# Gated cross-attention with experts: x and the experts' rows turned by VectorE out of 32-column quarters instead of by TensorE

## The chip, the core and the metric

The kernel runs on 1 core of one Trainium2 chip. A time is the device time of one execution in microseconds (us); the median of 3 runs is compared. One more execution is profiled, and all durations below come from it. TensorE (PE) multiplies, VectorE (DVE) and ScalarE (ACT) work on tiles in SBUF and PSUM, GpSimd (POOL) computes a little and issues the indexed transfers, and SyncE (SP) issues all other transfers, in the order in which its program names them.

## The reference, cut to what matters

```
x: (32, 128, 256)   ctx: (32, 128, 192)   16 heads of 64   8 experts, hidden 1024, capacity 1024
x = x + tanh(g_xattn) * attention(layernorm(x), ctx)          # Wq, Wk, Wv, Wo, bo
xf = layernorm(x) as (4096, 256)
each row goes to its two best experts' lists (first choices first, at most 1024 rows an expert)
h  = relu(rows @ fc1.T + b1);  eo = h @ fc2 + b2              # for each expert
x  = x + tanh(g_ffn) * sum over its two experts of gate * eo
```

All in float32. The kernel splits each float32 operand of a product into a high part (float32r) and the rest and adds three products.

## The kernel before, in words

**Attention.** The 32 batches are worked on in 8 groups `g` of 4 batches (`GB`), 512 tokens (`TOK`). A group has 8 steps `j`, one for each pair of heads; step `u = 8 g + j`. In step `u` TensorE turns the probabilities of step `u - 2`, makes the queries, the next keys and values, the scores of step `u`, and weighs values for step `u - 2`. VectorE takes maxima of the scores, copies turned probabilities out of PSUM, and scales probabilities (`scale_probs`, in two halves `hh`); ScalarE takes exponentials, which need the maxima. Single steps carry more (`misc_of`, line 77): `O0`, `O1` (output projection of the group before, step 2), `XA`, `XB`, `LT`, `LX`, `PR` (routing of the group before, steps 3 to 6), and in step 7 `FA` and `FB`: 4 transposes each, which turn the next group's normalised x, `xn`, into a PSUM bank (`front`, line 578). ScalarE then copies the bank to `xT_h`, VectorE subtracts to `xT_l` (line 1136), and the next query waits for both (`s_f_split`, line 523). `xn` itself is normalised by VectorE in place in step 5 (groups 0 and 1) or 4 (line 956). VectorE's order in step 7 is: maxima of the step before, `probs_out`, `scale_probs` half 0, `attention_low`, `route_slots` (from group 1 on), `scale_probs` half 1, the two subtractions for `xT_l`.

SP's order in the attention is a list by hand: `iteration(g, nxt, has_prev)` (line 282) loads x of group g + 1, the context of group g + 2, the x rows for the residual (into `rows[:, 1]`), and stores the finished x. After `iteration(0)` SP issues one transfer of 8256 KB that fills `disp`, the experts' lists in DRAM, with blanks (line 305); it waits for nothing but a memset.

**Experts.** 8 experts, each in two halves of 512 rows: groups `n = 0 .. 15`. A group has an up part (8 tiles `m` of 6 products of 512 columns), then 8 transposes that turn the rows of group n + 1 from `rows[half]` into the PSUM banks `rT` (`transpose_rows`, line 1353, called at line 1400), then a down part (96 products of 256 columns). ScalarE applies the Relu of each up tile, copies `rT` to `rT_h` (`high_rows`) and, once for each expert, copies the next expert's weights (`split_high`). VectorE splits `hid`, subtracts for `rT_l` (`low_rows`), subtracts for the weights (`split_low`), and writes the scaled result `eo`. GpSimd adds `eo` into the output by index. SP's `step(e, nxt, par)` (line 1285) loads the weights of expert `nxt` (`load_expert`), its biases, and then the rows of both halves, each of which waits until VectorE has read the tags of group n (`s_meta`), so the rows of group n + 2 are asked for at the start of group n.

## Time and profile before

| | us |
|---|---|
| median of 3 runs (lowest, highest) | 948.61 (948.35, 949.02) |
| the profiled execution | 951.25 |
| its span | 949.5 |
| PE busy | 930.2, 98% of the span |
| DVE, ACT, POOL busy | 651.6, 515.6, 276.7 |
| granted TensorE clock, mean | 0.997 of full |

The profiled execution took 951.25 us, 1.75 us more than the span from its first to its last instruction, and 2.64 us more than the median. Busy time of PE is modelled for pipelined products, so the step from one PE instruction's start to the next is what a product costs, and not its listed length.

### The profile page before, as it was taken

How to read it: one execution, taken by the hardware profiler on the slowest of the kernel's cores; microseconds unless marked ns; L12 is line 12 of the kernel's file. 1: busy time of each engine (PE TensorE's matmuls, PEld its weight loads, DVE VectorE, ACT ScalarE, POOL GpSimd, SP SyncE). 2: the span in 40 equal slices, each digit the busy share in tenths (PEclk: the TensorE clock that was granted, in tenths of full speed). 3: DMA queues.
4: the chain of work that ended last, by engine and by line, in shares of the span. 5: the costliest groups of instructions: out<-in, count | busy, mean ns of one | idle time of the engine just before them, and what ended most of it. 6: DMA issues, size and time to landing. Idle time of an engine off the chain costs nothing.

```text
span 949.5 us, 19031 instructions
## 1 busy us (share of the span) xinstructions
PE 930.2 (98%) x7224; PEld 813.0 (86%) x7224; DVE 651.6 (69%) x1536; ACT 515.6 (54%) x1608; POOL 276.7 (29%) x300
## 2 busy tenths in 40 slices
PE   8999999999999999999999999999999999999996
PEld 6788889889889888888898877999999999999995
DVE  4884895895885886867847747665757575757552
ACT  5774684784783774755847624343434343535331
POOL 4911133133133233243022250223232323232222
PEclk9999999999999999999999999999999999999998
DMA  9196320120021021012011015525252626252222
GB/s 250 36 295 141 111 68 29 40 73 34 30 79 57 1 79 58 14 58 65 13 35 46 33 70 169 139 45 139 46 142 42 148 43 148 45 146 48 29 23 23
DMA packets 61019, 73.36 MB, mean 77 GB/s; under 512 B 5870, under 2 KB 53781, under 8 KB 60928
## 3 DMA queue, kind: packets, MB, share of 16 engines
q1 hardware_dynamic: 48640, 55.89, 19.7%
q0 software_dynamic: 12288, 16.25, 9.5%
q8 instruction: 58, 0.95, 0.4%
q14 instruction: 33, 0.27, 0.1%
HBM read 43.23 MB, written 29.49 MB: 77 GB/s over the span
## 4 chain that ended last, share of the span: by engine, by line
PE 92%; DVE 2%; ACT 1%; issue 1%; DMA 1%; POOL 1%; another core or an unknown queue 0%; POOLq 0%; DVEq 0%; SPq 0%
PE out_bank L603 6%; PE probT L590 6%; PE down L1411 6%; PE down L1413 6%; PE down L1412 6%; PE score L615 6%; PE up L1395 6%; PE up L1394 6%; PE up L1396 6%; PE query_bank L531 3%; PE query_bank L533 3%; PE query_bank L532 3%; PE key_bank L557 3%; PE rT L1358 1%; PE key_bank L549 1%; PE key_bank L551 1%
## 5 line engine op out<-in xcount | busy, mean ns | idle before, releaser
L1447 ACT ACTIVATE hid<-up,b 128x512 f32<-128x512 f32 x124 | 85.4, 690 | 199.1 <-PE up L1396 126.1
L1330 POOL DMA_INDIRECT out_dram<-eo,index x64 | 99.7, 1559 | 274.9 <-DVE eo L1517 246.2
L1067 DVE TENSOR_REDUCE negmax<-score 128x4 f32<-128x512 f32 x128 | 82.3, 685 | 41.1 <-PE score L615 41.0
L430 POOL DMA_INDIRECT disp<-packed,slots x56 | 58.3, 1041 | 159.8 <-DMA disp<-packed,slots 105.7
L805 ACT ACTIVATE k_sb<-key_bank 128x512 f32<-128x512 f32 x64 | 38.7, 605 | 118.1 <-PE key_bank L557 116.9
L853 ACT ACTIVATE probs_odd<-score,negmax 128x128 f32<-128x128 f32 x256 | 91.3, 383 | 20.8 <-DVE negmax L1067 20.8
L853 ACT ACTIVATE work<-score,negmax 128x128 f32<-128x128 f32 x256 | 91.5, 385 | 16.7 <-DVE negmax L1067 16.1
L1508 DVE TENSOR_TENSOR hid_l<-hid,hid_h 128x512 fp32r<-128x512 f32 x128 | 88.7, 693 | 4.4
L1075 DVE COPY pT<-probT 128x512 f32<-128x512 f32 x128 | 82.3, 685 | 13.7 <-PE probT L590 13.5
L1517 DVE SCALAR_TENSOR_TENSOR eo<-down,gate,shares_b 128x256 f32<-128x256 f32 x64 | 29.6, 481 | 85.5 <-PE down L1413 85.5
L1506 DVE CAST hid_h<-hid 128x512 fp32r<-128x512 f32 x128 | 54.8, 428 | 37.6 <-ACT hid L1447 36.7
L615 PEld LDWEIGHTS score<-k_sb,q_sb 64*128 64x128 f32 x1024 | 66.7, 187 | 5.6 <-ACT q_sb L805 3.1
L1411 PE MATMUL down<-w_split,hid_h 128*128 128x256 f32 x256 | 71.3, 279 | 0.0
L1411 PE MATMUL down<-w_h,hid_h 128*128 128x256 f32 x256 | 71.3, 279 | 0.0
L1413 PE MATMUL down<-w_split,hid_l 128*128 128x256 f32 x256 | 70.7, 276 | 0.0
L1413 PE MATMUL down<-w_h,hid_l 128*128 128x256 f32 x256 | 70.7, 276 | 0.0
L1412 PE MATMUL down<-w_l,hid_h 128*128 128x256 f32 x256 | 70.7, 276 | 0.0
L1412 PE MATMUL down<-w_split,hid_h 128*128 128x256 f32 x256 | 70.7, 276 | 0.0
L603 PE MATMUL out_bank<-pT,v_sb 128*64 128x128 f32 x1008 | 68.9, 279 | 0.7 <-DVE aT_l L937 0.5
L615 PE MATMUL score<-k_sb,q_sb 64*128 64x128 f32 x1024 | 68.5, 273 | 1.0 <-ACT q_sb L805 0.9
L603 PEld LDWEIGHTS out_bank<-pT,v_sb 128*64 128x64 f32 x1008 | 53.7, 136 | 8.4 <-DVE aT_l L937 0.7
L853 ACT ACTIVATION_READ_ACCUMULATOR work<-score,negmax 128x1 f32 x256 | 57.3, 224 | 0.0
(314 smaller groups left out, 2753.6 us busy)
## 6 DMA issues: line engine op xcount, KB each, us to landing
disp<-fixed SPq DMA_DIRECT2D x1, 8256.0 KB, 34.2
rows<-disp SPq DMA_DIRECT2D x16, 516.0 KB, 5.0
rows<-x_dram SPq DMA_DIRECT2D x16, 512.0 KB, 5.2
w_raw<-fc1T_dram SPq DMA_DIRECT2D x8, 1024.0 KB, 8.0
w_raw<-fc_dram SPq DMA_DIRECT2D x8, 1024.0 KB, 10.7
out_dram<-rows SPq DMA_DIRECT2D x8, 512.0 KB
c_raw<-ctxT_dram SPq DMA_DIRECT2D x8, 256.0 KB, 4.4
c_raw<-ctxT_dram SPq DMA_DIRECT2D x16, 128.0 KB, 4.9
```

The source lines that it names most:

```text
L430: pool.indirect_dma_start(out=disp[:, :], out_offset=bass.IndirectOffsetOnAxis(ap=slots[:, j, b:b + 1], axis=0), in_=rows_[:, b, :], in_of ...
L603: last = mm(bank[hh * DH:(hh + 1) * DH, b * P:(b + 1) * P], v_sb[:, j // 4, b, cols], pT[:, hh, b * P:(b + 1) * P], start=True, stop=True)
L615: last = mm(score[hh][:, t], q_sb[r, t], k_sb[u % 2][r, t], start=True, stop=True)
L853: last = nc.scalar.activation(probs[w % 2][:, c, :], score[hh][:, b * P:(b + 1) * P], ACT.Exp, bias=negmax[:, w % 2, c:c + 1], accum_out=s ...
L1067: V.tensor_reduce(negmax[:, w % 2, hh * GB:(hh + 1) * GB], score[hh][:, :].rearrange("p (i k) -> p i k", i=GB), axis=AX, op=ALU.max, negat ...
L1075: V.tensor_copy(pT[:, hh, :], probT[hh][:, :]).then_inc(pt_done, 1)
L1330: pool.indirect_dma_start(out=out_rows[:, :], out_offset=bass.IndirectOffsetOnAxis(ap=index[half][:, i:i + 1], axis=0), in_=eo[half][:, i, ...
L1411: mm(o, hid_h[:, k, t], w2_h[par][:, k, :], start=(k == 0), stop=False)
L1412: mm(o, hid_h[:, k, t], w2_l[par][:, k, :], start=False, stop=False)
L1413: last = mm(o, hid_l[:, k, t], w2_h[par][:, k, :], start=False, stop=(k == HK - 1))
L1447: nc.scalar.activation(hid[m % 2][:, :], up_bank(n, m)[:, :], ACT.Relu, bias=b1[par][:, m:m + 1]).then_inc(s_hid, 1)
L1508: V.tensor_tensor(hid_l[:, m, :], hid[m % 2][:, :], hid_h[:, m, :].bitcast(f32), ALU.subtract).then_inc(s_hid_split, 1)
```

## The change

Both places where TensorE turns rows lose their transposes, apart from the first group of rows of the experts. In their place SP brings the data in 32-column quarters. For 512 rows and 256 columns there are 8 transfers; each takes 32 columns (128 bytes) of all 512 rows, and lays them on 32 partitions such that row `32 t + s` lands on partition `s`, block `t`. `V.transpose` of VectorE, which turns 32 by 32 blocks, then makes of it the operand with columns on partitions.

For the attention, `xn` must first go to DRAM: `regroup(g)` stores it to `normal`, waits until that has landed, and issues the 8 loads into `blocks`, which is the memory of `rows[:, 1]`. SP calls it in its order behind the fill of `disp` (group 0), and behind `iteration(g)`. VectorE turns both halves in step 7, ahead of `scale_probs` half 1. For the experts, `load_rows` issues 9 transfers instead of one: 8 quarters and the tags. The loads and subtractions of the weights are parted into first and second layer, of which the second moves to an expert's second half.

```diff
 def misc_of(u):
     g, j = divmod(u, NP)
-    if j == NP - 1:
-        return ["FA", "FB"] if g < NG - 1 else []
...
         def iteration(g, nxt, has_prev):
             if nxt is not None:
-                sp.wait_ge(s_f_ready, 2 * g + 2)
+                if g == 0:
+                    sp.wait_ge(s_f_ready, 2)
+                else:
+                    sp.wait_ge(s_normal_out, 16 * g)
                 load_x(nxt, 0, s_x_in)
...
                     sp.wait_ge(s_o_done, 2 * g - 2)
+                sp.wait_ge(s_turned, DK * g)
                 load_x(g - 1, 1, s_xr_in)
                 store(g - 1, g)
+
+        def regroup(g):
+
+            sp.wait_ge(s_xn_ready, g + 2)
+            sp.dma_start(normal.rearrange("(b p) d -> p b d", p=P), xn).then_inc(s_normal_out, 16)
+            if g > 0:
+                sp.wait_ge(s_o_done, 2 * g)
+            sp.wait_ge(s_normal_out, 16 * (g + 1))
+            for k in range(DK):
+                for q in range(P // SQ):
+                    d = slice(k * P + q * SQ, k * P + (q + 1) * SQ)
+                    sp.dma_start(blocks[q * SQ:(q + 1) * SQ, k, :].rearrange("s (t d) -> s t d", d=SQ),
+                                 normal[:, d].rearrange("(t s) d -> s t d", s=SQ)).then_inc(s_blocks_in, 16)
...
         sp.dma_start(disp.rearrange("(t p) w -> p t w", p=P),
                      blank[:, :].unsqueeze(1).to_broadcast([P, E * CAP // P, W])).then_inc(s_blank_out, 16)
+        regroup(0)
         iteration(1, 2, True)
+        regroup(1)
...
         for g in range(2, NG - 1):
             iteration(g, g + 1, True)
+            regroup(g)
@@ attention, ScalarE, step @@
-            if "FA" in kinds:
+            if g < NG - 1 and u % NP == NP - 1:
                 for k in range(DK):
-                    act.wait_ge(s_f_ready, 2 * g + 3 + k)
-                    high(xT_h[:, k, :], (query_bank, probT[1])[k][:, :]).then_inc(s_f_hi, 1)
+                    act.wait_ge(s_turned, DK * g + k + 1)
+                    high(xT_h[:, k, :], xn2T[:, k, :]).then_inc(s_f_hi, 1)
@@ attention, VectorE, step @@
             if has_prev and j == 7:
                 route_slots(route, g, g)
+            if has_next and j == NP - 1:
+                dve.wait_ge(s_blocks_in, 16 * DK * (P // SQ) * (g + 1))
+                dve.wait_ge(s_q_ready, NP * (g + 1))
+                for k in range(DK):
+                    V.transpose(xn2T[:, k, :], blocks[:, k, :]).then_inc(s_turned, 1)
             if u > 0:
                 scale_probs(u - 1, 1)
@@ experts, SP, step and load_rows @@
             if first:
                 sp.wait_ge(s_e0_lo, 2)
+                load_expert(sp, fc1T, fc2, nxt, w1_raw, w2_raw, s_w_in, s_w2_in)
             else:
+                sp.wait_ge(s_w1_lo, e)
+                load_first_layer(sp, fc1T, nxt, w1_raw, s_w_in)
                 sp.wait_ge(s_w_lo, e)
-            load_expert(sp, fc1T, fc2, nxt, w1_raw, w2_raw, s_w_in)
+                load_second_layer(sp, fc2, nxt, w2_raw, s_w2_in)
...
                 sp.wait_ge(s_meta, n + 1)
+                if n > 0:
+                    sp.wait_ge(s_turned, 2 * n)
                 load_rows(nxt, half)

         def load_rows(e, half):
             src = disp_v[bass.ds(e, 1), half * TOK:(half + 1) * TOK, :]
-            sp.dma_start(rows[half][:, :, :], src.rearrange("o (i p) w -> p (o i) w", p=P)).then_inc(rows_in[half], 16)
+            for k in range(DK):
+                for q in range(P // SQ):
+                    d = slice(k * P + q * SQ, k * P + (q + 1) * SQ)
+                    sp.dma_start(blocks[half][q * SQ:(q + 1) * SQ, k, :].rearrange("s (t d) -> s t d", d=SQ),
+                                 src[:, :, d].rearrange("o (t s) d -> s (o t) d", s=SQ)).then_inc(rows_in[half], 16)
+            sp.dma_start(tags[half][:, :, :], src[:, :, D:W].rearrange("o (i p) w -> p (o i) w", p=P)).then_inc(rows_in[half], 16)
@@ experts, TensorE, group @@
-            if n < LAST:
-                transpose_rows(16 * (e + 1) if half == 0 else 16 * (e + 2), 1 - half)
@@ experts, VectorE, group @@
+        def turn_rows(n):
+
+            dve.wait_ge(rows_in[n % 2], loads_of(n))
+            for k in range(DK):
+                V.transpose(turned[:, k, :], blocks[n % 2][:, k, :]).then_inc(s_turned, 1)
...
             if n < LAST:
+                turn_rows(n + 1)
                 low_rows(n + 1)
-            if half == 0 and e < E - 1:
-                split_low(e + 1, 1 - par)
+            if e < E - 1:
+                (split_first_layer, split_second_layer)[half](e + 1, 1 - par)
```

ScalarE's `high_rows` and VectorE's `low_rows` read `turned` in SBUF instead of `rT` from group 1 on, and ScalarE's `split_high` waits for each layer's weights by itself.

## Rows read from the trace of the kernel before

**Rows 1.** The page: busy time of the engines, and the chain by engine.

```profile
PE 930.2 (98%) x7224; PEld 813.0 (86%) x7224; DVE 651.6 (69%) x1536; ACT 515.6 (54%) x1608; POOL 276.7 (29%) x300
PE 92%; DVE 2%; ACT 1%; issue 1%; DMA 1%; POOL 1%; another core or an unknown queue 0%; POOLq 0%; DVEq 0%; SPq 0%
```

**Rows 2.** Busy time by stretch: one group of the experts (columns: stretch, length, engines, clock).

```profile
633.40:656.30 22.90, 22.90 (x156) 20.95 (x155) 17.13 (x30) 11.78 (x17) 6.27 (x4) 1.00 0.48 120
```

**Rows 3.** Timeline of PE between an up and a down part (start, length, line).

```profile
610.43 1.03 PE L1358 MATMUL rT<-ident,rows 128*128 128x128 f32 x8
611.23 0.28 PE L1410 MATMUL down<-w_split,hid_h 128*128 128x64 f32 x1
```

**Rows 4.** Timeline of PE, group 2, step 7.

```profile
264.86 0.39 PE L569 MATMUL value_bank<-wv_h,c_l 128*128 128x512 f32 x1
265.09 0.39 PE L570 MATMUL value_bank<-wv_d,c_d 128*128 128x512 f32 x1
265.48 0.66 PE L580 MATMUL query_bank<-ident,rows 128*128 128x128 f32 x4
...
266.50 0.50 PE L557 MATMUL key_bank<-c_d,wk_e 64*128 64x512 f32 x1
```

**Rows 5.** Timeline of VectorE, group 2, steps 4 to 8 (brackets: idle before).

```profile
243.65 1.38 DVE L956 TENSOR_SCALAR rows<-rows,mv,rstd 128x256 f32<-128x256 f32 x4
...
260.83 1.27 DVE L1067 TENSOR_REDUCE negmax<-score 128x4 f32<-128x512 f32 x2
...
268.96 1.28 DVE L1067 TENSOR_REDUCE negmax<-score 128x4 f32<-128x512 f32 x2
...
273.10 0.18 DVE L1080 RECIPROCAL rsum<-sums 128x4 f32<-128x4 f32 x1 [0.26 <-ACT probs_odd L853]
```

**Rows 6.** Timeline of PE: the scores of the first step of group 3.

```profile
273.61 1.16 PE L615 MATMUL score<-k_sb,q_sb 64*128 64x128 f32 x16
```

**Rows 7.** Timeline of VectorE, group 0, steps 5 to 8.

```profile
50.23 1.37 DVE L956 TENSOR_SCALAR rows<-rows,mv,rstd 128x256 f32<-128x256 f32 x4
...
63.88 0.68 DVE L937 TENSOR_TENSOR aT_l<-out_bank,aT_h 128x512 fp32r<-128x512 f32 x1
...
67.03 1.28 DVE L1067 TENSOR_REDUCE negmax<-score 128x4 f32<-128x512 f32 x2
```

**Rows 8.** Timeline of PE: the scores of the first step of group 1.

```profile
72.44 1.05 PE L615 MATMUL score<-k_sb,q_sb 64*128 64x128 f32 x16
```

**Rows 9.** Timeline of SP: the fill of `disp`, and the next load of x.

```profile
46.86 0.59 SPq L305 DMA_DIRECT2D disp<-fixed  x1
65.62 6.10 SPq L243 DMA_DIRECT2D rows<-x_dram  x1
```

**Rows 10.** DMA of the stretch 64 to 66.5: issues with KB and us to landing.

```profile
rows<-x_dram SPq DMA_DIRECT2D x1, 512.0 KB, 17.5
```

**Rows 11.** The page: DMA issues, KB each, median us to landing.

```profile
disp<-fixed SPq DMA_DIRECT2D x1, 8256.0 KB, 34.2
rows<-disp SPq DMA_DIRECT2D x16, 516.0 KB, 5.0
```

**Rows 12.** DMA of the stretch 750 to 752, one bias load alone (slices of 0.05 us).

```profile
DMA  0000000000000000000000000000000023321000
...
q1 hardware_dynamic: 144, 0.00, 3.6%
...
b<-fc1b_dram SPq DMA_DIRECT2D x1, 4.0 KB, 1.6
```

**Rows 13.** Timeline of VectorE, group 1: x normalised in step 5, slots in step 7.

```profile
116.74 1.38 DVE L956 TENSOR_SCALAR rows<-rows,mv,rstd 128x256 f32<-128x256 f32 x4
...
132.82 0.17 DVE L1058 TENSOR_TENSOR slots<-slot,late 128x8 uint32<-128x8 f32 x1
```

**Rows 14.** Timeline of SP: rows of expert 1 asked for (two issues, the last at the end).

```profile
578.93 22.36 SPq L1302 DMA_DIRECT2D rows<-disp  x2
```

More of the change, by code:

```diff
@@ L90, in gated_block @@
     disp = nc.dram_tensor("disp", [E * CAP, W], f32, kind="Internal").ap()
+    normal = nc.dram_tensor("normal", [TOK, D], f32, kind="Internal").ap()
     x_v = x.rearrange("b p d -> p b d")
@@ L116, in gated_block @@
         with ExitStack() as ctx:
-            attention(nc, ctx, block, sem, x_v, out_v, disp, ctxT, g_x, g_f, wq, wk, wv, wo, bo, gateT, fc1T, fc2, shared)
+            attention(nc, ctx, block, sem, x_v, out_v, disp, normal, ctxT, g_x, g_f, wq, wk, wv, wo, bo, gateT, fc1T, fc2, shared)
         with ExitStack() as ctx:
@@ L125, in keep_warm, with load_first_layer, load_second_layer, load_expert @@
         nc.tensor.matmul(bank[:, 0:rhs.shape[-1]], lhsT, rhs, start=True, stop=True)
-def load_expert(sp, fc1T, fc2, e, w1_raw, w2_raw, done_sem):
+def load_first_layer(sp, fc1T, e, w1_raw, done_sem):
     sp.dma_start(w1_raw[:, :, :], fc1T[bass.ds(e, 1), :, :].rearrange("o (k p) h -> p (o k) h", p=P)).then_inc(done_sem, 16)
+def load_second_layer(sp, fc2, e, w2_raw, done_sem):
     sp.dma_start(w2_raw[:, :, :], fc2[bass.ds(e, 1), :, :].rearrange("o (k p) d -> p (o k) d", p=P)).then_inc(done_sem, 16)
-def attention(nc, ctx, block, sem, x_v, out_v, disp, ctxT, g_x, g_f, wq, wk, wv, wo, bo, gateT, fc1T, fc2, shared):
+def load_expert(sp, fc1T, fc2, e, w1_raw, w2_raw, done1, done2):
+    load_first_layer(sp, fc1T, e, w1_raw, done1)
+    load_second_layer(sp, fc2, e, w2_raw, done2)
+def attention(nc, ctx, block, sem, x_v, out_v, disp, normal, ctxT, g_x, g_f, wq, wk, wv, wo, bo, gateT, fc1T, fc2, shared):
     f32, f32r, i32, u32 = mybir.dt.float32, mybir.dt.float32r, mybir.dt.int32, mybir.dt.uint32
@@ L160, in attention @@
     xn, xr, x1 = (rows[:, n] for n in range(3))
+    blocks = rows[:, 1].rearrange("p b d -> p (b d)").rearrange("p (k t) -> p k t", k=DK)
     flat_rows = rows.rearrange("p a b d -> p a (b d)")
@@ L214, in attention @@
         "dve_self", "pool_self", "dve_gate", "pool_gate", "e0_in", "c0_hi", "e0_hi", "gc_ready", "gc_done",
-        "shift", "shift2", "before", "lt_ready", "lt_done", "second", "minus_mean", "pair_in", "beat",
+        "shift", "shift2", "before", "lt_ready", "lt_done", "second", "minus_mean", "pair_in", "beat", "normal_out", "blocks_in", "turned",
     ))
@@ L731, in step @@
             if w >= 0:
-                if kinds[1:] and kinds[1] != "FB":
+                if kinds[1:]:
                     pe.wait_ge(*misc_done(kinds[1], u // NP))
@@ L1241, in experts @@
     shares_b2 = sb("shares_b2", [P, GB, D])
-    rows = [sb("rows_0", [P, GB, W])]
-    sb("line_up_rows", [P, 96 // 4])
-    rows.append(sb("rows_1", [P, GB, W]))
+    first_rows = sb("first_rows", [P, GB, W])
+    blocks = [sb(f"blocks_{n}", [P, DK, TOK]) for n in range(2)]
+    turned = sb("turned", [P, DK, TOK])
+    tags = [sb(f"tags_{n}", [P, GB, W - D]) for n in range(2)]
     b2 = [sb(f"b2_{n}", [P, D]) for n in range(2)]
@@ L1351, in _, with transpose_first @@
         mm = nc.tensor.matmul
-        def transpose_rows(loads, half):
-            pe.wait_ge(rows_in[half], loads)
+        def transpose_first():
+            pe.wait_ge(s_first_rows, 16)
             for k in range(DK):
                 for b in range(GB):
-                    last = nc.tensor.transpose(rT[k][:, b * P:(b + 1) * P], rows[half][:, b, k * P:(k + 1) * P], ident[:, :])
+                    last = nc.tensor.transpose(rT[k][:, b * P:(b + 1) * P], first_rows[:, b, k * P:(k + 1) * P], ident[:, :])
                 last.then_inc(s_rt_ready, 1)
@@ L1436, in high_rows @@
             for k in range(DK):
-                act.wait_ge(s_rt_ready, 2 * n + k + 1)
-                nc.scalar.activation(rT_h[:, k, :], rT[k][:, :], ACT.Copy).then_inc(s_rt_hi, 1)
+                if n == 0:
+                    act.wait_ge(s_rt_ready, k + 1)
+                    src = rT[k][:, :]
+                else:
+                    act.wait_ge(s_turned, 2 * n - 1 + k)
+                    src = turned[:, k, :]
+                nc.scalar.activation(rT_h[:, k, :], src, ACT.Copy).then_inc(s_rt_hi, 1)
         def group(n, e, par, half):
@@ L1471, in meta @@
         def meta(n, e, half):
-            dve.wait_ge(rows_in[half], 16 * (e + 1))
+            if n == 0:
+                dve.wait_ge(s_first_rows, 16)
             if not (isinstance(e, int) and e == 0):
                 dve.wait_ge(scatters[half], 16 * GB * e)
-            weight = rows[half][:, :, D + 1]
+            tag = first_rows[:, :, D:W] if n == 0 else tags[half][:, :, :]
+            weight = tag[:, :, 1]
             me.enter(3 * n)
-            V.tensor_copy(index[half][:, :], rows[half][:, :, D])
+            V.tensor_copy(index[half][:, :], tag[:, :, 0])
             i = me.mark(V.tensor_scalar(den[:, :], weight, 1.0, None, ALU.add))
```

50 lines of the change are left out of this document (24 added, 26 removed).

## The prediction

> **What bounds the kernel now.** I read the page first: PE is busy for 98% of the span, and the chain that ended last runs 92% through PE [rows 1]. So an instruction taken from PE gives back what it costs there, as long as no other engine's work comes late for it. Then I read stretches and timelines. In the experts a group of 22.9 us has 22.9 us of PE, 17.13 us of VectorE and 11.78 us of ScalarE [rows 2]: PE bounds, with 5 us to spare on VectorE. In step 7 of an attention group it is otherwise. From the maxima at 260.83 to those at 268.96 VectorE works for 8.1 us without an idle bracket, and idles again only from 272.84 [rows 5]. Those maxima are late: ScalarE's exponentials follow them, and the scores of the next step at 273.61 [rows 6] follow the exponentials, 4.65 us behind the start of the maxima. The reader is to see two bounds: PE in the experts, VectorE in steps 7 of groups 1 to 6. SP's list gives the third thing to look at: the fill of `disp` is issued at 46.86 and lands 34.2 us later [rows 9, 11], at 81.1.
>
> **What comes off PE.** In the experts the 8 transposes cost PE 611.23 - 610.43 = 0.80 us [rows 3], not the 1.03 listed, since products overlap. They go from 15 groups: 15 x 0.80 = 12.0 us. They covered the time from the last up tile to its split halves, but the down part begins with tile 0, split long before, and its tile 7 comes after 42 further products; so no wait takes their place. In step 7 of the attention two products start 0.23 us apart; the last value product starts at 265.09, so ends its turn at 265.32, and the next non-transpose starts at 266.50 [rows 4]: `FA` and `FB` cost 1.18 us. Seven of these are at most 8.3 us, if PE is what bounds there.
>
> **What comes onto VectorE.** Two `V.transpose` of 128 x 512 float32 for each group. The trace has none. Nearest are a float32 subtraction of the same size, listed 0.68 [rows 7] but 0.60 apart from the next instruction, and a 128 x 256 normalisation, 4 of them in 1.38 us, so 0.35 each [rows 5], 0.70 for two. I take 0.60 each, 1.2 us a group, with 0.8 and 1.5 as ends. In the experts VectorE goes from 17.1 to 18.3 us in a group's 22.1, and the second layer's subtraction moves from the fuller half to the emptier one, so the load is more even still: cost nothing. The cover is those 4 to 5 us of idle; without it each group would lose 1.2. ScalarE has 11 us idle a group [rows 2], which also covers weights for expert 1 that arrive later behind the nine row transfers. The sources in SBUF instead of PSUM change no duration that I can read.
>
> In groups 1 to 6 of the attention the turn stands ahead of `scale_probs` half 1, in the stretch in which VectorE never idles. So the maxima at 268.96 start 1.2 us later, and with them exponentials and scores. That PE comes 1.18 us earlier to its waits is worth nothing, since it waits for VectorE: 6 x 1.2 = +7.2 us, not -7.1. Ends: +4.8 and +9.
>
> The microarchitecture page of the Trainium skill (Vector Engine (DVE) Microarchitecture Reference, section 3.8) says that the transpose mode sustains one element a cycle and lane. At the skill's 0.96 GHz that would be an estimate of 0.53 us for 512 elements, and the sum for six groups 6.4 instead of 7.2. No row here shows the operation.
>
> **What comes onto the queue.** `regroup(0)` is behind the fill of `disp` in SP's list. Its x is normalised at 50.23 + 1.37 = 51.6 [rows 7], so the store of `normal` is issued at about 52, when the fill has 29 us to go. Does it wait for the fill? The load of x issued at 65.62, which needs nothing, took 6.1 us to issue and landed after 17.5 us, at 83.1 [rows 9, 10]; alone such a transfer takes about 5.0 [rows 11]. It landed just behind the fill. The store has the same size and stands at the same place of the queue, so it lands at about 83. Only then SP issues the 8 loads.
>
> Those 8 loads are 4096 packets of 128 bytes. Nearest in size are the 128 packets of 32 bytes of a bias load: they pass in 6 slices of 0.05 us, so 2.3 ns each over all 16 engines, which are then busy to a quarter, and the load lands after 1.6 us [rows 12]. At that pace 4096 take 9.6, and with 1.6 for landing 11 us. Below lies SP's own issue, 0.4 to 0.6 us each [rows 9]: 8 x 0.5 + 1.6 = 6 us. Above lie 512 packets of 1032 bytes, 5.0 us to landing [rows 11], so 3.4 without the 1.6: 8 x 3.4 + 1.6 = 29 us. I take 8.5, between the first two, since 128 bytes are nearer to 32 than to 1032. So the blocks are in at T = 83 + 8.5 = 91.5.
>
> VectorE reaches the turn at 63.88 + 0.60 = 64.5 [rows 7] and stands there, with `scale_probs` half 1 behind it, and PE's transposes of these probabilities behind that. After T: two turns 1.2, a scaling of 0.8 (a reciprocal of 0.18 [rows 5] and an operation as long as a subtraction), two subtractions 1.2, then the 4.65 us from maxima to scores: T + 7.9. Before, these scores started at 72.44 [rows 8]. The delay is T - 64.5 = 27.0 us, with 24.5 (T = 89) and 47.5 (T = 112) as ends. PE, idle that long, may come back at the lower of its two clocks; its query, keys and values before the scores are 15 products of 0.23 us, 3.4 us, so 6.8 at half speed against the 4.65 of the others: at most 2 us more, in the range.
>
> Group 1: x is normalised at 118.12, the turn is due at 132.99 [rows 13], 14.9 us for a store (2.2 us at the fill's 8256 KB in 34.2 us, plus 1.6 to land, 4) and the loads (8.5): 12.5, so 2.4 us to spare. At 11 us for the loads it is even, at 29 it loses 18. Groups 2 to 6 normalise a step earlier: x is done at 245.03, and the turn is due 2.0 us ahead of the maxima at 268.96 [rows 5]: 21.9 us of room. They lose only from 18 us of loads on. In the experts rows are asked for 31.5 us before PE turned them (578.93 to 610.43) [rows 3, 14], with a new set each group. Nine transfers of 512 packets at 2.3 ns take 10.6 us of a 22 us group: hidden. From 4.3 ns a packet on, nine transfers fill the group and the rest of the traffic does not fit.
>
> **The sum.** -12.0 (experts) + 7.2 (groups 1 to 6) + 27.0 (group 0) = +22.2 us. On the profiled execution's 951.25 that is 973.45; the median of the runs is 2.6 lower, which gives **971 us**.
>
> **Rivals.**
>
> Turn covered. PE's 1.18 us is gained in groups 1 to 6 and VectorE's 1.2 costs nothing, because something in the stretch from 260.83 gives way: -7.1 in place of +7.2, 957 us. Against it: no idle bracket in the stretch [rows 5]. For it: the scores follow after 4.65 us, in which waits could shrink.
>
> Packets dear. Each 512-packet quarter costs as a row transfer does, 3.4 us. Group 0 then loses 47.5, group 1 18, groups 2 to 6 11 each, and nine transfers of 3.4 make 31 us for a group of the experts, 36 with the weights (two loads of 1 MB for two groups) against 22: +14 in 14 groups. Together about +316 us, near 1265; halfway, with 15 us for the loads, 981. Against it: the engines were a quarter busy with small packets [rows 12]. For it: nothing in the trace reads 128 bytes at a stride. The DMA page of the skill (DMA: Bandwidth & Descriptors, Rules for kernel authors) speaks against this change: it calls a plain transfer with a rearranged access pattern 19 times slower than the hardware's own turn. By that rule the time would be in the hundreds above; here runs of 128 bytes stay whole.
>
> No queue behind the fill (the other side, faster). The store slips past the fill, in 4 us, and the blocks are in at 52 + 4 + 8.5 = 64.5, just when the turn is due. Then only +7.2 - 12.0 remain, -4.8: 944 us. It decides from T = 69 on down. Against it: the load of x at 65.62 [rows 10].
>
> **Chances.** Forecast as summed, 958 to 990: 0.62. Turn covered, about 957: 0.12. Packets dear, over 990: 0.12. No queue: 0.10. The rest, 0.04, is a sum that ends near no change. Range: both ends of the forecast, the covered turn, and a loss of 5 more for dearer packets: 953 to 993. A difference under 0.2% (1.9 us) is no change here. Faster 0.10, the same 0.03, slower 0.87.
>
> **What would show it.** Right: VectorE with an idle of 25 us or more before its first transpose, ended by a transfer, in group 0 alone; PE idle for as long from about 67; maxima of step 7 in later groups about 1.2 us later against the group's start, and groups of the experts of 22.1 us. Wrong: a turn in group 0 that starts before 70; groups of the experts longer than 22.9, with VectorE waiting for blocks; a `V.transpose` far from 0.6 us; or waits before the turn in groups 2 to 6.

## The result, and the profile after

The changed kernel takes 961.61 us (median, 961.45 to 962.66) where the kernel before takes 948.48 us in the same series: **13.1 us slower, ratio 1.014, 95% interval 1.0123 to 1.0158**. The forecast was 971 with a range of 953 to 993. The profiled execution took 962.66 us with a span of 960.9, 11.4 more than the span of before (949.5).

The page first: busy time, then the chain that ended last by engine and, in part, by line.

```profile
PE 913.7 (95%) x7048; PEld 795.6 (83%) x7048; DVE 678.6 (71%) x1580; ACT 520.0 (54%) x1608; POOL 282.2 (29%) x300
PE 76%; DVE 13%; DMA 4%; ACT 3%; issue 2%; POOL 1%; SPq 0%; POOLq 0%; DVEq 0%
```

Against [rows 1] PE lost 16.5 us of work and 3 points of its share: the span grew although the fullest engine has less to do. The chain says who is in the way now, and not what it costs: VectorE went from 2% to 13%, transfers from 1% to 4%.

The transfers are one place. Timeline of SP, group 0 (start, length, line):

```profile
46.63 0.59 SPq L330 DMA_DIRECT2D disp<-fixed  x1
51.43 19.04 SPq L311 DMA_DIRECT2D normal<-rows  x1
78.46 4.04 SPq L318 DMA_DIRECT2D rows<-normal  x8
```

and of VectorE:

```profile
63.67 0.68 DVE L956 TENSOR_TENSOR aT_l<-out_bank,aT_h 128x512 fp32r<-128x512 f32 x1
84.34 1.30 DVE L1151 STREAM_TRANSPOSE work<-rows 128x512 f32<-128x512 f32 x2 [19.99 <-DMA rows<-normal]
```

The store of `normal` is issued at 51.43 and only at 78.46, 27.0 us later, SP goes on to the 8 loads; the turn starts at 84.34, 5.9 us behind them, after 20.0 us of idle. PE then shows this (timeline of PE, the same place):

```profile
66.79 0.66 PE L616 MATMUL probT<-ident,work 128*128 128x128 f32 x4
86.48 1.12 PE L616 MATMUL probT<-ident,work 128*128 128x128 f32 x4 [19.04 <-DVE work L1101]
...
90.90 0.63 PE L578 MATMUL key_bank<-c_l,wk_h 128*128 128x512 f32 x1
91.33 0.63 PE L579 MATMUL key_bank<-c_h,wk_l 128*128 128x512 f32 x1
91.75 0.48 PE L580 MATMUL key_bank<-c_d,wk_d 128*128 128x512 f32 x1
92.08 0.39 PE L595 MATMUL value_bank<-wv_h,c_h 128*128 128x512 f32 x1
92.31 0.39 PE L596 MATMUL value_bank<-wv_l,c_h 128*128 128x512 f32 x1
...
93.44 1.05 PE L641 MATMUL score<-k_sb,q_sb 64*128 64x128 f32 x16
```

PE stands for 19 us behind `scale_probs` half 1. When it comes back its products start 0.43 us apart (90.90, 91.33, 91.75) and from 92.08 on 0.23. The stretches name the clock (stretch, length, busy time of PE, its weight loads, VectorE, ScalarE and GpSimd, granted clock, DMA share, GB/s):

```profile
60.00:70.00 10.00, 7.44 (x66) 5.84 (x62) 3.98 (x6) 3.88 (x18) 3.11 (x3) 1.00 1.10 323
70.00:84.00 14.00, 0.00 (x0) 0.00 (x0) 0.00 (x0) 0.00 (x0) 0.00 (x0) 0.55 0.79 192
84.00:93.00 9.00, 6.34 (x18) 4.74 (x18) 7.98 (x15) 6.07 (x22) 2.67 (x3) 0.56 0.55 174
```

The granted clock is 1.00 (2.4 GHz) up to 70, 0.55 while PE does nothing, and mostly still the lower level (1.2 GHz) when it starts again. The scores of step 8 start at 93.44, against 72.44 [rows 8].

The other place shows when the first scores of each group are set beside those of before, from the two timelines of PE:

| first scores of group | before | after | later by |
|---|---|---|---|
| 0 | 20.86 | 20.66 | -0.20 |
| 1 | 72.44 | 93.44 | 21.00 |
| 2 | 139.57 | 161.76 | 22.19 |
| 3 | 206.59 | 229.96 | 23.37 |
| 4 | 273.61 | 298.16 | 24.55 |
| 5 | 340.64 | 366.36 | 25.72 |
| 6 | 407.66 | 434.56 | 26.90 |
| 7 | 474.57 | 501.56 | 26.99 |
| 7, last step | 533.19 | 560.29 | 27.10 |

(The prediction's rows call the group whose step 7 ends at 273.61 group 2; counted from 0, as here, it is group 3. Its own group 1 is the group that starts at 72.44 in both counts. The counts of groups, 1 to 6, are not affected.) So the end of group 0 costs 21.2 us (21.00 and the 0.20 by which the kernel had started earlier), each of groups 1 to 5 costs 1.18, and group 6, with a step behind it, about 0.2. Within a group of the middle all 1.18 falls at one place: the scores of step 7 come 1.11 earlier than in before (PE no longer transposes x ahead of them) and the scores that follow come 2.29 later. Timeline of VectorE in that place, after, group 3:

```profile
286.78 1.74 DVE L1101 TENSOR_TENSOR work<-work,rsum 128x512 f32<-128x512 f32 x1
288.44 0.68 DVE L956 TENSOR_TENSOR aT_l<-out_bank,aT_h 128x512 fp32r<-128x512 f32 x1
...
290.31 1.30 DVE L1151 STREAM_TRANSPOSE work<-rows 128x512 f32<-128x512 f32 x2
291.54 0.13 DVE L1099 RECIPROCAL rsum<-sums 128x4 f32<-128x4 f32 x1
291.70 0.69 DVE L1101 TENSOR_TENSOR work<-work,rsum 128x512 f32<-128x512 f32 x1
292.31 1.28 DVE L956 TENSOR_TENSOR xT_l<-work,xT_h 128x512 fp32r<-128x512 f32 x2
293.52 1.28 DVE L1086 TENSOR_REDUCE negmax<-score 128x4 f32<-128x512 f32 x2
```

There is no bracket of idle. The two turns take 1.23 us to the next instruction; and the same scaling by the same shapes is listed 1.74 us at 286.78 and 0.69 at 291.70.

From the last scores to the first transposes of the experts it is 39.60 us after and 42.02 before. The experts: their down parts start 21.91 us apart (634.23 and 656.14), against 22.79 before (611.23 to 634.01, and the same for nearly all). The busy row of the stretch, one group:

```profile
634.23:656.14 21.91, 21.91 (x147) 20.02 (x146) 16.02 (x30) 8.34 (x14) 6.18 (x4) 1.00 0.56 118
```

Timeline of VectorE, the turn in the same group:

```profile
635.61 0.69 DVE L1563 TENSOR_TENSOR hid_l<-hid,hid_h 128x512 fp32r<-128x512 f32 x1
636.22 1.30 DVE L1536 STREAM_TRANSPOSE turned<-blocks 128x512 f32<-128x512 f32 x2
637.63 1.29 DVE L1542 TENSOR_TENSOR rT_l<-turned,rT_h 128x512 fp32r<-128x512 f32 x2
```

No wait for blocks stands before the turn, and PE is still full, so the quarters of rows are in time and PE's saving is whole. The sum of the parts: 21.2 (group 0) + 5.9 (groups 1 to 5) + 0.2 (group 6) - 2.4 (between attention and experts) - 13.3 (experts) = +11.6 us, where the spans differ by 11.4; the missing 0.2 is the earlier start of group 0.

### The profile page after: what moved, and what is told of

The parts are those of the page before. It is cut to its first block, busy times and chain, and to the rows that moved or that the text cites. A ratio compares the mean times of both kernels' runs of the same rounds, so it can differ in the third digit from the quotient of the medians.

```text
span 960.9 us, 18925 instructions
## 1 busy us (share of the span) xinstructions
PE 913.7 (95%) x7048; PEld 795.6 (83%) x7048; DVE 678.6 (71%) x1580; ACT 520.0 (54%) x1608; POOL 282.2 (29%) x300
## 4 chain that ended last, share of the span: by engine, by line
PE 76%; DVE 13%; DMA 4%; ACT 3%; issue 2%; POOL 1%; SPq 0%; POOLq 0%; DVEq 0%
PE down L1448 6%; PE down L1449 6%; PE down L1450 6%; PE up L1435 6%; PE up L1434 6%; PE up L1436 6%; PE score L641 5%; PE out_bank L629 4%; PE probT L616 4%; DMA normal<-rows 3%; DVE pT L1094 2%; PE query_bank L559 2%; PE query_bank L561 2%; PE query_bank L560 2%; ACT probs_odd L872 2%
## 5 line engine op out<-in xcount | busy, mean ns | idle before, releaser
L559 PE MATMUL query_bank<-xT_h,w_split 128*128 128x512 f32 x128 | 56.3, 440 | 3.7 <-DVE xT_l L956 3.7
## 6 DMA issues: line engine op xcount, KB each, us to landing
disp<-fixed SPq DMA_DIRECT2D x1, 8256.0 KB, 30.5
```

Source lines behind the costliest of these rows:

```text
L559: mm(query_bank[:, :], wq_h[:, k, c], xT_h[:, k, :], start=(k == 0), stop=False)
```

## Experiments

Each time is a median beside the kernel before in the same series; what counts is the difference to it. On that scale the whole change is +13.1.

| kernel | time | before | difference | ratio, 95% interval |
|---|---|---|---|---|
| experts' half alone | 937.22 | 950.47 | -13.3 | 0.986, 0.9844 to 0.9877 |
| attention's half alone | 977.16 | 950.47 | +26.7 | 1.0278, 1.0261 to 1.0295 |
| fill behind `regroup(0)` | 948.72 | 950.47 | -1.8 | 0.9985, 0.9975 to 0.9994 |
| no split of the context | 957.54 | 950.47 | +7.1 | 1.0074, 1.0057 to 1.0091 |
| fill in ScalarE's queue | 959.75 | 948.99 | +10.8 | 1.0114, 1.0097 to 1.0131 |
| 16 loads in group 0 (a single run) | 968.23 | 948.99 | +19.2 | none |
| a third turn | 969.84 | 948.99 | +20.9 | 1.0223, 1.0206 to 1.024 |
| split later | 959.47 | 948.99 | +10.5 | 1.0103, 1.0086 to 1.012 |
| late fill | 943.41 | 951.00 | -7.6 | 0.9919, 0.9903 to 0.9936 |
| late fill, split later | 937.10 | 951.00 | -13.9 | 0.985, 0.9833 to 0.9866 |
| experts' half, split later | 935.01 | 951.00 | -16.0 | 0.9833, 0.9817 to 0.985 |

### The two halves apart

Experts' half: the function `attention` and `misc_of` of before, the function `experts` of after. Attention's half: the other way round. In the texts put on record "theory" is what was expected and "rival" what would come out if it were wrong; "the scale of 948.5" means 948.5 plus the difference.

> The experts' half of the change alone; the attention, with FA and FB on TensorE, is that of before. Theory: the experts' groups shrink from 22.79 to 21.91 us as in after, 15 x 0.88 = 13.2 us, and nothing else moves: 948.5 - 13.2 = 935.3. In after the finish phase between attention and experts was 2.4 us shorter as well; if that came with the experts' code, 933. Rival (the attention's loss and the experts' gain are not independent, part of the 13.2 is time that the late start gave): a gain well under 10 us.

> The attention's half of the change alone; the experts are those of before. Theory: +21.2 us in group 0, +5.9 in groups 1 to 5, +0.2 in group 6, no gain behind it: 948.5 + 27.3 = 975.8, or 973.4 if the finish phase's 2.4 us are of the attention's half. Rival as for the experts' half alone: the two parts do not add up to +13.1.

Measured -13.3 and +26.7, together +13.4 where the whole change is +13.1: the halves add up, and each is what the trace gave it. From the first transposes of the experts to the end of the span it is 361.0 us in the experts' half and in the whole change (361.01), and 374.3 in the attention's half and in before (949.5 - 575.21 = 374.3): 13.3 us for 15 groups, 0.89 each. The 2.4 us between attention and experts follow neither half: this phase takes 41.6 us with the one, 40.8 with the other, and between 39.5 and 42.1 over all thirteen profiles. One piece of it is an idle of ScalarE for which the trace has no releaser on this core; before has it (timeline of ScalarE):

```profile
540.92 0.60 ACT L805 ACTIVATE aT_h<-out_bank 128x512 fp32r<-128x512 f32 x1 [2.10 <-remote]
```

The attention's half has it too, and the whole change, with the same attention, has not. The eight profiles that have this idle take 40.4 to 42.1 us for the phase, the five that have not take 39.5 to 39.7. What it depends on was not tried, and stays open.

### Where the fill stands

```diff
-        sp.wait_ge(s_blank, 1)
-        sp.dma_start(disp.rearrange("(t p) w -> p t w", p=P),
-                     blank[:, :].unsqueeze(1).to_broadcast([P, E * CAP // P, W])).then_inc(s_blank_out, 16)
         regroup(0)
+        sp.wait_ge(s_blank, 1)
+        sp.dma_start(disp.rearrange("(t p) w -> p t w", p=P),
+                     blank[:, :].unsqueeze(1).to_broadcast([P, E * CAP // P, W])).then_inc(s_blank_out, 16)
         iteration(1, 2, True)
```

> Changed from after: the fill of disp stands behind regroup(0) in SP's list instead of ahead of it, nothing else. Theory (the 20.0 us idle of VectorE in group 0 is the store of normal standing behind the 8 MB fill): the store lands within about 4 us of its issue at 51.4, the 8 loads within 6 more, the blocks are in near 61 and the turn is not late at 63.9. The step from group 0 to group 1 then costs what it costs in groups 1 to 5 (+1.2 us against before) and not +22.1 - 0.9: the median goes from 961.6 to about 942. The x of group 2 and the residual's x then land behind the fill, near 95, which may take back 1 to 3 us in group 1. Rival (the two dependent trips through DRAM take 30 us by themselves, whatever stands ahead): the turn stays near 84 and the time near 961.

Timeline of SP with the fill behind the loads:

```profile
50.89 0.38 SPq L311 DMA_DIRECT2D normal<-rows  x1
55.76 4.06 SPq L318 DMA_DIRECT2D rows<-normal  x8
59.86 0.49 SPq L331 DMA_DIRECT2D disp<-fixed  x1
60.40 22.73 SPq L251 DMA_DIRECT2D rows<-x_dram  x1
```

and of VectorE:

```profile
63.73 1.29 DVE L1151 STREAM_TRANSPOSE work<-rows 128x512 f32<-128x512 f32 x2
...
98.86 0.75 DVE L1113 SCALAR_TENSOR_TENSOR rows<-query_bank,fixed,rows 128x512 f32<-128x512 f32 x1 [14.40 <-POOL rows L440]
```

The store now takes 4.9 us (50.89 to 55.76) instead of 27.0, and the turn at 63.73 waits for nothing. The first scores of group 1 are at 71.57, with group 0's own start 0.77 earlier than in before: the stall is gone, and the place costs -0.1. But the kernel gets only 14.9 us of the 19.6 expected (-1.8 against +13.1). Its timeline has the rest in group 1: step 11 is 6.6 us longer than in before, by the starts of the scores. The residual's x stands behind the fill now, GpSimd adds the bias to it at 96.06, and VectorE, waiting for GpSimd, reaches the residual at 98.86. I had given this 1 to 3 us. The stall was moved from one customer of the transfers to another.

Is it the order in SP's queue that holds them, or the engines that are full? The same fill from ScalarE's queue, issued at 45.02, 1.6 us earlier than SP had issued it (SP's own issue of it is left out):

```diff
@@ attention, ScalarE, end of a step @@
+            if u == 4:
+                act.wait_ge(s_blank, 1)
+                act.dma_start(disp.rearrange("(t p) w -> p t w", p=P),
+                              blank[:, :].unsqueeze(1).to_broadcast([P, E * CAP // P, W])).then_inc(s_blank_out, 16)
```

> Changed from after: the fill of disp is issued by ScalarE at the end of its step 4 (near 46.0, where SP issued it at 46.6), so it moves at the same time through the same 16 engines but in another queue. Theory (order inside SP's queue held the store of normal): store and loads pass beside the fill, the turn of group 0 is at 64 to 68, and the x of group 2 and the residual's x are no longer behind the fill either: 961.6 - 20 = 941.6, on the scale of the run of before at 948.5. Rival (the engines are full of the fill, whichever queue it stands in): the store still lands near 78, turn at 84, 961.

Timeline of SP in that kernel:

```profile
51.50 0.38 SPq L311 DMA_DIRECT2D normal<-rows  x1
61.65 13.24 SPq L318 DMA_DIRECT2D rows<-normal  x8
```

and of VectorE:

```profile
81.55 1.31 DVE L1152 STREAM_TRANSPOSE work<-rows 128x512 f32<-128x512 f32 x2 [17.13 <-DMA rows<-normal]
```

My theory gave 941.6, the rival 961; it came out at +10.8, which is 959.3 on the scale of 948.5. So the queue theory is only half of it. The store did pass the fill in part: 10.15 us instead of 27.0, so the order in the queue held it for the difference. But the stretch from the store's landing to the turn grew from 5.9 to 19.9 us. The fill landed after 35.9 us, at 80.9, and the turn starts at 81.55, just behind it: the loads now share the engines with what is left of the fill (DMA share 1.14 from 61.6 to 74.9, against 0.67 while the whole change has its loads, 78.5 to 84.3). Whether it is the engines or the memory behind them that is full, no run here tells. The turn came 2.8 us earlier than in the profile of the whole change, and 4.5 earlier than in that of the third turn (86.07), which is of this series. The Trainium skill (Trainium Kernel Development and Optimization, Key Constraints) says that DMAs of the SP, ACT and POOL queues run on the same 16 engines and interleave, and that several issuing engines only save issue time. This run agrees: SP's issue of the store fell from 19.04 us to 0.38, and the turn is at 81.55 against 84.34.

What the fill itself takes differs between profiles, and the stall follows it. In those with the fill in its old place and the store behind it, it landed after 30.5 us (the whole change), 30.9 (attention's half), 30.6 (no split), 32.6 (third turn), 32.8 (split later) and 33.0 (16 loads), and the loads were begun at 78.46, 78.40, 78.33, 80.05, 80.54 and 80.70. In before it was 34.2 [rows 11], in the two kernels with the experts' half alone 32.4 and 34.8. The difference goes with the series: attention's half and no split were measured in one (30.9, 30.6), third turn, split later and 16 loads in the next, on another chip (32.6 to 33.0). So a kernel of the second series has some 2 us more of stall than the whole change had, and the subtraction of before does not take that out, as nothing in before stands still for the fill. The whole change was not measured again in that series.

Last, the fill where nothing asks for transfers soon: behind the residual's x of group 0, which puts it in group 1, with GpSimd's wait for its end (`dispatched(0)`) moved to group 1 as well. `fill()` is the wait and the transfer of before, and they are gone from their old place.

```diff
                 load_x(g - 1, 1, s_xr_in)
+                if g == 1:
+                    fill()
                 store(g - 1, g)
@@ attention, GpSimd, iteration @@
                 rstd(mv2, var2, rstd2, s_stats2, g, s_rstd2)
+            if g == 1:
+                dispatched(0)
             if g < NG - 2:
...
                 split_ctx(g + 2)
-            if g == 0:
-                dispatched(0)
```

> Changed from after: the fill of disp is issued behind the residual's x of group 0 (near 70, in group 1), and GpSimd waits for its end later in group 1, so neither the store and loads of the turned blocks nor the x of group 2 nor the residual's x share the engines with it. Theory (two steps: the fill's traffic made the stall of group 0, and with the fill moved only a little it fell on the residual's x, 6.6 us in group 1): group 0 costs -0.1, group 1 no more than the others, groups 1 to 5 1.18 each, group 6 0.2: 948.5 + 6.0 - 13.2 = 941.3. Rival (the fill hits another transfer wherever it stands): 945 to 950.

Timeline of SP with the late fill:

```profile
56.18 4.06 SPq L325 DMA_DIRECT2D rows<-normal  x8
60.28 0.49 SPq L251 DMA_DIRECT2D rows<-x_dram  x1
...
65.37 0.38 SPq L251 DMA_DIRECT2D rows<-x_dram  x1
65.79 0.51 SPq L292 DMA_DIRECT2D disp<-fixed  x1
```

Measured -7.6, so 940.9 on the scale of 948.5; expected 941.3. The fill is issued at 65.79, only 6 us later than in the first experiment, behind both loads of x. The step from group 0 to group 1 costs -0.1, group 1 no more than the others. The stall in group 0 cost 13.1 + 7.6 = 20.7 us by the times (21.3 by the two profiles), and all of it comes back.

### The loads of the quarters

In group 0 alone each load is cut in two along the blocks: 16 issues with the same packets.

```diff
-                    sp.dma_start(blocks[q * SQ:(q + 1) * SQ, k, :].rearrange("s (t d) -> s t d", d=SQ),
-                                 normal[:, d].rearrange("(t s) d -> s t d", s=SQ)).then_inc(s_blocks_in, 16)
+                    dst = blocks[q * SQ:(q + 1) * SQ, k, :].rearrange("s (t d) -> s t d", d=SQ)
+                    src = normal[:, d].rearrange("(t s) d -> s t d", s=SQ)
+                    if g > 0:
+                        sp.dma_start(dst, src).then_inc(s_blocks_in, 16)
+                    else:
+                        for t in (slice(0, TOK // SQ // 2), slice(TOK // SQ // 2, TOK // SQ)):
+                            sp.dma_start(dst[:, t], src[:, t]).then_inc(s_blocks_in, 16)
```

VectorE's wait counts the 8 loads more.

> Changed from after: in group 0 each of the 8 loads of the turned blocks is issued as two of half the packets, so 16 issues with the same 4096 packets and bytes; groups 1 to 6 as in after. Theory (SP's issue of 0.5 us a transfer sets the pace, the packets themselves fit into it): 8 more issues, the turn starts 4 us later, at 88.3, and the time is 4 us longer, 965.6. Rival (the 4096 packets of 128 bytes set the pace): the turn stays at 84.3, the time at 961.6.

Timeline of SP with the 16 loads:

```profile
80.70 7.74 SPq L324 DMA_DIRECT2D rows<-normal  x16
```

and of VectorE:

```profile
89.86 1.31 DVE L1156 STREAM_TRANSPOSE work<-rows 128x512 f32<-128x512 f32 x2 [25.71 <-DMA rows<-normal]
```

From the start of the loads to the turn it is 9.16 us instead of 5.88, so 3.3 more for the same 4096 packets, and SP's issue grew by 3.7 (7.74 against 4.04). The pace is SP's, half a microsecond an issue; the last quarter lands 1.8 us after SP is done, with 16 issues 1.4. The time is one run's, +19.2 against +13.1: of these 6.1 us 3.3 are the issues and 2.2 the later landing of the store behind this profile's longer fill (80.70 against 78.46); 0.6 stay open.

### What bounds step 7 in groups 1 to 6

A third turn, of the first half, into a tile that nothing reads:

```diff
+                if g > 0:
+                    dve.wait_ge(s_junk, g - 1)
+                    V.transpose(junk[:, :], blocks[:, 0, :]).then_inc(s_junk, 1)
                 for k in range(DK):
```

> Changed from after: in groups 1 to 6 VectorE turns the first half of the blocks once more, into a tile that nothing reads, ahead of the two turns. Theory (VectorE bounds step 7 in these groups): each group is longer by one turn, 0.61 us, 6 x 0.61 = +3.7 us: 965.3 on the scale of before at 948.5, and the step from step 7 to the next step 0 grows from +2.29 to +2.90. Rival (the 1.18 us a group is a wait of PE for something else, GpSimd's or ScalarE's part, with VectorE idle in it): under +1 us.

The step in which the scores came 2.29 us later than in before is now 2.92 in four of the groups 1 to 5, 3.81 in one, and in group 6 1.90 instead of 1.28. So one more turn costs 0.62 us in each: whatever VectorE gets here, the group pays. The time was +20.9, 4 us above what was expected: 0.9 is the one group, 2.1 is group 0 with the longer fill of this series (32.6 against 30.5), and about 1 I can't place.

Why is group 6 cheap? In its step 7 GpSimd doesn't split a context. Elsewhere it does, beside VectorE. Timeline of GpSimd, the whole change, group 3:

```profile
284.63 1.28 POOL L401 TENSOR_TENSOR c_l<-c_raw,c_h 128x512 fp32r<-128x512 f32 x1
285.89 0.69 POOL L402 TENSOR_SCALAR c_t<-c_t,lower_half 128x512 fp32r<-128x512 f32 x1
286.67 1.29 POOL L405 TENSOR_TENSOR c_d<-c_raw,c_t 128x512 fp32r<-128x512 f32 x1
```

The last one runs from 286.67 to 287.96, and the scaling that VectorE starts at 286.78 takes 1.74 us instead of 0.69, as if it began when GpSimd ended. Its neighbours, maxima and copies whose source is in PSUM, keep their times beside GpSimd (1.27 for two, at 284.19 and at 285.39). First the split left out in groups 1 to 5, so that the later groups work with the context of earlier ones and the result isn't the reference's; then the whole split, moved:

```diff
                 pool.wait_ge(s_k_ready, NP * (g + 1))
-                split_ctx(g + 2)
+                if g == 0:
+                    split_ctx(g + 2)
+                else:
+                    pool.wait_ge(s_c_in, 48 * (g + 3))
+                    pool.sem_inc(s_c_ready, 1)
```

> Changed from after: GpSimd's split of the context (five operations of 128 x 512, 5.1 us) is left out in groups 1 to 5, so the later groups compute with the context of groups 1 and 2; waits, counts and all other work stay. Theory (the split runs beside VectorE's scaling of the probabilities in step 7, lists it at 1.74 us instead of 0.69, and this makes VectorE the bound there): the scaling falls to 0.69, each of groups 1 to 5 costs what group 6 costs (about +0.2 instead of +1.18), and the time falls by 5 us, to 956.6. Rival (VectorE's row of work in the stretch is what bounds, with or without GpSimd): the groups still cost 1.1 to 1.2 us each, 961.6.

```diff
-                pool.wait_ge(s_k_ready, NP * (g + 1))
+                pool.wait_ge(s_k_ready, NP * (g + 1) + 2)
                 split_ctx(g + 2)
```

> Changed from after: GpSimd's split of the context waits for two more key products, so it runs some 13 us later, in the first steps of the next group, whole and with the reference's result. Theory (as for the kernel without the split, which took the groups' cost from 1.18 to 0.00): groups 1 to 5 cost nothing, group 0 1.2 less too: 961.6 - 7 = 954.6, if the loads of the context and of the residual's x, which stand behind the split in SP's list, still come in time. Rival (the delay reaches the residual's x, and with it the residual at step 2, which waits for GpSimd's bias): no gain or a loss of up to 5 us in each group.

Timeline of VectorE, group 3, split later:

```profile
287.18 0.69 DVE L1101 TENSOR_TENSOR work<-work,rsum 128x512 f32<-128x512 f32 x1
...
289.67 1.30 DVE L1151 STREAM_TRANSPOSE work<-rows 128x512 f32<-128x512 f32 x2
```

Without the split the later half of the step falls from +2.29 to +1.10 in all five groups, against the -1.11 ahead of it: the groups' cost is 0.0, and the time is +7.1, 6.0 us better than the whole change. With the split later the same +1.10 stands in four of five groups (1.45 in one). Its time is +10.5, a gain of 2.6 and not the 7 expected: the attention gives 5.4 us in groups 1 to 5, but with this series' fill of 32.8 us group 0 cost 3.0 more (2.1 of it the later landing of the store), and the 1.2 us expected there can't come, since what VectorE saves in group 0 it waits longer for the blocks. Its runs lie between 957.7 and 960.3, wider than those of the others. The clean reading is the pair with the late fill, below. The collision itself is moved and not gone: in the next group the scalings at 297.23 and 301.74 are listed 1.11 and 1.03, and still four of the five groups cost no more than with no split at all.

The Trainium skill (SBUF — State Buffer, section SBUF: two separate sides) says that GpSimd and a VectorE operation with two SBUF inputs take one shared port pair as an exclusive lock, and that whoever comes second waits for the whole instruction of the first. The rows agree: GpSimd's subtraction starts 0.11 us ahead of the scaling, the scaling has both inputs in SBUF and ends 1.05 us late, and with GpSimd elsewhere it is 0.69.

### Both losses taken away

> The late fill and GpSimd's later split of the context together, on the whole change. Theory: the two losses of the attention are separate and both go: 941.3 - 5.9 = 935.4 on the scale of before at 948.5, with up to 0.7 more in group 0, where the scaling ran beside the split too: 934.7 to 935.4, as fast as the experts' half of the change alone (935.3), so the attention's half is worth nothing even with its losses gone. Rival (TensorE's 1.18 us a group come back once nothing holds VectorE): 935.4 - 7 = 928.

> The experts' half of the change alone, with GpSimd's later split. Theory (before, the contended scaling cost step 7 of groups 1 to 5 0.18 us against group 6, since TensorE takes over as the bound there): 935.3 - 5 x 0.18 = 934.4, hardly to be told from 935.3. Rival (VectorE bounded step 7 of before by the whole second that the contention takes): 935.3 - 5.9 = 929.4.

The chain by engine of the whole change with both edits:

```profile
PE 80%; DVE 12%; ACT 4%; issue 2%; POOL 1%; DMA 1%; another core or an unknown queue 0%; POOLq 0%; DVEq 0%; SPq 0%
```

and of the experts' half with the later split:

```profile
PE 92%; DVE 2%; ACT 1%; issue 1%; DMA 1%; POOL 1%; another core or an unknown queue 0%; POOLq 0%; DVEq 0%; SPq 0%
```

VectorE still has 12% of the first chain although the time is 14 us shorter than before, and 2% of the second, as in before: the share says where the chain runs, the time what that costs.

The first measured -13.9, 934.6 on the scale of 948.5, as expected (934.7 to 935.4), and 6.3 better than with the late fill alone. At the end of the attention it stands 0.5 us ahead of before: with both losses gone the attention's half is worth nothing beside the experts' half alone (-13.3), since its groups go on costing 1.10 in the second place and giving 1.11 in the first. The rival (928) is out: VectorE holds the place even with the 1.05 us back. The second measured -16.0, 932.5, and 934.4 was expected. Its last scores start 3.1 us earlier than in before, of which 0.6 is its earlier start; the other 2.5 are 0.19 at the place where I expected it and 0.27 in the steps on either side of it (0.16 and 0.11) in each of the five groups, and 0.2 in group 6. It is the fastest of all kernels here, and it leaves the attention's x with TensorE. Both were measured in one series, 937.10 and 935.01, and their runs don't overlap: with both losses taken away the attention's half still costs about 2 us, since the later split helps the kernel without it too.

## Why the prediction was right, point by point

**The direction and its cause** were right: group 0 waits for a transfer that comes late because of the fill, once, and this outweighs the gain in the experts. The late fill shows it: 20.7 us come back. The size was too large by 10.6 us (+22.2 summed, +11.6 by the same terms in the trace), and the four differences all lie on one side: 5.8 in group 0, 1.1 in groups 1 to 6, 1.3 in the experts, 2.4 in the finish. None made good for another. Of the signs named, the idle of 25 us or more came at 20.0 on VectorE and 19.0 on PE; the others came as stated.

**Group 0's size, 27.0, was too large: 21.2 measured.** The sum was T + 7.9 with T = 91.5. T was 84.34. Of the 7.2 us, 4.5 are the store: it landed at 78.46 and not at 83, and 3.7 of that is a fill that took 30.5 us and not 34.2 [rows 11]. One execution had been read as if the fill always took as long; over the six profiles with the store behind it it took 30.5 to 33.0. The other 2.6 are the loads: 5.9 us, at the lower bound of 6 that SP's issue gave, where I had taken 8.5. Choosing by packet size was the mistake: the small packets never set the pace, the issues did. (The 0.4 to 0.6 us for an issue are more than [rows 9] show, which have one of 0.59; the eight took 0.50 each.) Against these, the stretch from turn to scores was 9.1 us and not 7.9, as PE was back at the lower clock; the text had put up to 2 us for it into the range and 0 into the sum. With the fill behind the loads and no stall ahead, the same stretch is 7.84 (63.73 to 71.57).

**The mechanism behind T was half told.** The text says that the store waits behind the fill in SP's queue. The run with the fill in ScalarE's queue shows that out of the queue the same transfers still come nearly as late, as they share the engines with it. The rival "no queue behind the fill" would have failed even if the queue were free.

**Groups 1 to 6: 7.2 forecast, 6.1 measured**, 1.18 in five and 0.2 in the sixth. VectorE bounds the place, as the text read from the missing idle brackets [rows 5]; the turn is 0.61 us, as the subtraction's distance had it (0.60). The Trainium skill's one element a cycle (Vector Engine (DVE) Microarchitecture Reference, section 3.8) made an estimate of 0.53; the trace has 0.61 from instruction to instruction, and no run here shows what the difference is. What the text didn't see is a part of why VectorE is full there: 1.05 us of one scaling is time lost to GpSimd, in before as well. The row stands in the timeline of before between those of [rows 5] (263.42, listed 1.73, its siblings 0.69):

```profile
263.42 1.73 DVE L1082 TENSOR_TENSOR work<-work,rsum 128x512 f32<-128x512 f32 x1
```

Group 6 has no such loss and nearly covered the turn.

**The experts: 12.0 forecast, 13.3 measured**, 0.89 a group and not 0.80. 0.80 is the distance from the first transpose to the next product. The rest stands behind that product, the first of the down part: in before the one that follows it starts 0.11 us later, in after 0.03 (timelines of PE, before, then after):

```profile
611.23 0.28 PE L1410 MATMUL down<-w_split,hid_h 128*128 128x64 f32 x1
611.34 0.36 PE L1411 MATMUL down<-w_split,hid_h 128*128 128x256 f32 x1
```

```profile
634.23 0.19 PE L1447 MATMUL down<-w_split,hid_h 128*128 128x64 f32 x1
634.26 0.36 PE L1448 MATMUL down<-w_split,hid_h 128*128 128x256 f32 x1
```

The covers held: no wait of VectorE for blocks, PE full, nine loads a group in time. VectorE's load is as even as the text had it: 12.71 and 17.02 us in two neighbouring groups before (from 611.23), 16.02 and 16.16 in the same two after (from 634.23).

**The turn covered, packets dear.** The first is out for groups 1 to 5 and came true for group 6. The second is out: 8 loads of 512 packets in 5.9 us, nine in each group of the experts without a wait. The Trainium skill (DMA: Bandwidth & Descriptors, Rules for kernel authors) gives a factor of 19 between a plain transfer with a rearranged pattern and the hardware's own turn; no run here has that turn, so the factor itself stays untried, but as a rule against this change it would need loads far slower than these 5.9 us.

**The finish** gave 2.4 us in the profiled pair that no term of the sum had. The profiles of the two halves give it to neither, and what it depends on stays open. Without it the traces would make the change 13.8 us slower, with it 11.4; the medians say 13.1.

## What to carry to other kernels

A transfer that work waits for has to be placed by what else is in the engines at that moment and not only by what stands ahead of it in its queue: here the remedy for a stall of 20.7 us was to issue a large background transfer some 19 us later, behind the small ones, while another queue for it brought the turn forward by 2.8 to 4.5. Before work is moved onto an engine, look whether its instructions of one shape all have one duration; one that is listed 2.5 times its siblings marks a place where the engine is held up already. What that costs only a run tells: taking the collision away gave 6.3 us with the turn beside it and, from -13.3 to -16.0 in two series, some 2.7 without. A gain on the fullest engine counts only in the stretches where that engine ends the waits: the same move, from TensorE to VectorE, gave 13.3 us in the experts and, with its losses mended, a loss of about 2 in the attention.

## What was unexpected about the hardware

- A fill of 8256 KB took 30.5 to 34.8 us to land in the nine profiles that issue it at the same place of SP's list, 30.6 and 30.9 in one series and 32.6 to 33.0 in the next for kernels with the same work ahead of it; 35.9 from ScalarE's queue beside the stores and loads.
- A store of 512 KB behind it took 27.0 us, beside it from another queue 10.15, and without it 4.9.
- Eight loads of 64 KB in packets of 128 bytes took 5.9 us alone, all of it issue but 1.8, and 19.9 beside the fill; SP's issue of them stretched from 4.04 to 13.24 us.
- VectorE's scaling with both inputs in SBUF took 1.74 us beside GpSimd's subtraction and 0.69 without it; operations with a source in PSUM in the same stretch kept their times (1.27 for two).
- After 19 us of idle PE ran its products 0.43 us apart up to 91.75 and 0.23 apart from 92.08; the granted clock was 0.55 in the idle and 0.56 from 84 to 93.
